# Naming the PSUM tiles of a local-attention block, and new orders for its five engines

## What is computed

```python
x = x + ga * attn_ref(layernorm(x) * (1 + ca) + sa, ...)      # causal part
h = layernorm(x) * (1 + cb) + sb
for i in range(6):                                             # the local layers
    h = attn_layer(shift_tokens(h), Wqkv[i], qs[i], ks[i], Wo[i]) + h
    h = ffn_layer(shift_tokens(h), ln_g[i], ln_b[i], W1[i], b1[i], W2[i], b2[i]) + h
return x + gb * h

# attn_layer: q, k = l2norm(.) * scale, rotary with a position scale;
#   windows of 32 keys, each query sees its own window and the one before;
#   softmax(8 q k^T) v, then @ Wo
# ffn_layer: a, gate = split(layernorm(x) @ W1 + b1); (a * gelu(gate)) @ W2 + b2
```

## Time and profile before

| | us |
|---|---|
| median of 3 runs | 3763.39 |
| the three runs | 3753.32, 3763.39, 3766.66 |
| the profiled execution, own time | 3756.22 |
| its span, first to last instruction | 3754.2 |
| PE busy | 3392.6 |
| POOL busy | 3107.4 |
| DVE busy | 2955.4 |
| ACT busy | 2601.3 |

### The profile page before, as it was taken

The page is one execution under the profiler, slowest core; times in us unless marked ns, Lnnn a source line. Parts: engine busy times, 40 slices in busy tenths (PEclk is TensorE's granted clock), DMA queues, the critical chain, the costliest instruction groups (busy, mean ns, idle before and its releaser), DMA issues.

```text
span 3754.2 us, 162428 instructions
## 1 busy us (share of the span) xinstructions
PE 3392.6 (90%) x72292; PEld 2052.2 (55%) x72292; DVE 2955.4 (79%) x3116; ACT 2601.3 (69%) x3315; POOL 3107.4 (83%) x2468
## 2 busy tenths in 40 slices
PE   7999999589998999989999889999899998989995
PEld 4666666355554555555555555555455555555553
DVE  7888887677887887878777778777788787887774
ACT  6777776467776666776677766776766777767773
POOL 3555556589998999989899988999899998989992
PEclk9999999799999999999999999999999999999997
DMA  1000000244545454545454544454444454545442
GB/s 62 5 5 8 5 5 24 75 112 114 122 107 118 95 117 108 117 109 116 93 127 108 117 100 106 114 122 105 113 102 110 116 116 106 119 95 116 104 108 80
DMA packets 162053, 347.53 MB, mean 93 GB/s; under 512 B 32588, under 2 KB 42064, under 8 KB 155088
## 3 DMA queue, kind: packets, MB, share of 16 engines
q1 hardware_dynamic: 161360, 337.15, 38.4%
HBM read 24.54 MB, written 4.19 MB: 8 GB/s over the span
## 4 chain that ended last, share of the span: by engine, by line
PE 50%; POOL 12%; DVE 7%; issue 6%; ACT 5%; SPq 1%; DMA 0%; DVEq 0%; POOLq 0%; ACTq 0%
PE psB L673 26%; PE psA L673 21%; POOL sq L1387 3%; PE psB L730 2%; DVE h L1289 2%; PE psA L730 1%; ACT sq L980 1%; POOL pb L1407 1%; POOL h L1382 1%; POOL h L1383 1%; POOL f_c L1412 1%; DVE ts L1281 1%; POOL n_a L1397 1%; POOL n_a L1394 1%; POOL n_b L1402 1%
## 5 line engine op out<-in xcount | busy, mean ns | idle before, releaser
L1362 POOL TENSOR_TENSOR pt<-wk,pt 128x256 f16<-128x256 f32 (+3 forms) x256 | 368.2, 1455 | 284.1 <-ACT pt L903 194.5
L1387 POOL TENSOR_TENSOR sq<-sq 128x512 f32<-128x512 f32 x384 | 487.3, 1281 | 82.7 <-ACT sq L980 82.4
L1382 POOL TENSOR_TENSOR h<-h,ts 128x512 f32<-128x512 f32 x384 | 503.1, 1310 | 35.3 <-DVE ts L1281 35.3
L1383 POOL TENSOR_TENSOR h<-h,ts 128x512 f32<-128x512 f32 x384 | 496.9, 1294 | 0.0
L1407 POOL TENSOR_TENSOR pb<-pb,rc 128x1024 f32<-128x1024 f32 x192 | 365.5, 1904 | 63.2 <-DVE rc L1302 60.5
L1300 DVE TENSOR_REDUCE sum<-pb 128x16 f32<-128x1024 f32 x192 | 232.9, 1213 | 108.5 <-ACT pb L1013 108.5
L1273 DVE TENSOR_TENSOR h<-psB,t_rot 128x1024 f32<-128x1024 f32 x192 | 233.6, 1217 | 77.1 <-ACT sq L980 72.6
L673 PE MATMUL psA<-kf,qf 64*32 64x64 f32 x18432 | 250.7, 227 | 29.3 <-issue 28.0
L980 ACT ACTIVATE sq<-psA 128x1024 f32<-128x1024 f32 x192 | 196.1, 1022 | 109.3 <-PE psA L673 109.2
L1273 DVE TENSOR_TENSOR h<-psA,t_rot 128x1024 f32<-128x1024 f32 x192 | 233.5, 1216 | 35.4 <-DMA kf<-h 13.9
L980 ACT ACTIVATE sq<-psB 128x1024 f32<-128x1024 f32 x192 | 196.2, 1022 | 88.2 <-PE psB L673 87.7
(11 more groups left out here) (364 smaller groups left out, 11040.7 us busy)
## 6 DMA issues: line engine op xcount, KB each, us to landing
qf<-h SPq DMA_DIRECT2D x768, 136.0 KB
kf<-h SPq DMA_DIRECT2D x768, 136.0 KB, 2.8
vev<-vo SPq DMA_DIRECT2D x192, 256.0 KB
vev<-vo SPq DMA_DIRECT2D x192, 224.0 KB
stage<-wqk SPq DMA_DIRECT2D x12, 512.0 KB, 5.3
stage<-wvl SPq DMA_DIRECT2D x12, 256.0 KB, 5.5
stage<-wof SPq DMA_DIRECT2D x6, 512.0 KB, 4.7
xb<-xt SPq DMA_DIRECT2D x8, 256.0 KB, 7.9
```

Of the source, the lines that this page charges most:

```text
L1362: e.tensor_tensor(pt[g][pr][:, :, 1, o:o + w], wk[(slot_of(s)[0] - 1) % SLOTS][:, :, 0:w], pt[g][pr][:, :, 0, o:o + w], ALU.subtract).then ...
L1382: e.tensor_tensor(halves_of(h, 0), halves_of(h, 0), t[1], ALU.subtract)
L1383: e.tensor_tensor(halves_of(h, 1), halves_of(h, 1), t[0], ALU.add).then_inc(ended["ad"])
L1387: e.tensor_tensor(sqb[c][:, 0, :], sqb[c][:, 0, :], sqb[c][:, 1, :], ALU.add).then_inc(ended["qa"])
```

## The change

Two things change.

**PSUM places.** The two rings are gone. A step now names its tile, A, B, C or D, which are psA0, psA1, psB0 and psB1. Four kinds of step that need only one bank (`ss`, `op`, `la`, `fo`) take one bank, the left (`l` or nothing) or the right (`r`), and wait only for the last users of that bank. A step that needs both banks waits for the last user of each. `plan_banks` in place of `plan_pairs` works that out, and `psum(s)` returns the bank or the pair.

**Orders.** All five tables are written anew. Nothing is added or removed: the same 2736 PE steps, 2088 of ACT, 2034 of DVE, 1536 of POOL and 492 of SP are there, in other places.

```diff
+ONE_BANK = ("ss", "op", "la", "fo")
-def plan_pairs(steps, rings):
-    at, had, place = {"A": 0, "B": 0}, {}, {}
+def plan_banks(steps, homes):
+
+    user, place = [None] * 8, {}
     for s in steps:
-        if s in rings:
-            r = rings[s]
-            slot = "AB".index(r) * 2 + at[r] % 2
-            at[r] += 1
-            place[s] = (slot, had.get(slot))
-            had[slot] = s
+        if s in homes:
+            at = 2 * "ABCD".index(homes[s][0]) + (homes[s][1:] == "r")
+            own = range(at, at + (1 if s[0] in ONE_BANK else 2))
+            place[s] = (at, sorted({user[i] for i in own if user[i]}))
+            for i in own:
+                user[i] = s
     return place
...
         def psum(s):
-            return pair[place[s][0]]
+            at = place[s][0]
+            return pair[at // 2][:, 512 * (at % 2):512 * (at % 2) + 512] if s[0] in ONE_BANK else pair[at // 2]
...
-                slot, before = place[s]
-                if before:
+                for before in place[s][1]:
...
 TENSOR = (
-    "f1:B+1 ss0:A+2 sc000:B+2 vp00:A+2 "
+    "f1:B vp01:D+1 ss0:Ar+1 sc000:B+1 vp00:D+1 sc003+1 sc002+1 sc001+1 pj10:C+1 ng00+1 sc010:A+1 sc013+1 sc012+1 "
...
 SYNC = (
-    "vd0 dm10 dm11 dm13 dm12 vd1 st1 dm00+1 dm01+1 dm03+1 st0+1 dm02+1 "
+    "dm10 st1 dm11 dm13 vd1 dm12 st0 dm00+1 dm01+1 dm03+1 dm02+1 vd0+1 "
```

More of the change, by code:

```diff
@@ L323, in program @@
         score_walk = [s for s in causal if s[0] == "c_sc"]
-        (tensor_walk, rings), (scalar_walk, _), (vector_walk, _), (gpsimd_walk, _), (sync_walk, _) = (
+        (tensor_walk, homes), (scalar_walk, _), (vector_walk, _), (gpsimd_walk, _), (sync_walk, _) = (
             walk(t) for t in (TENSOR, SCALAR, VECTOR, GPSIMD, SYNC))
@@ L330, in program @@
         count = ordinals((tensor_walk, scalar_walk, vector_walk, gpsimd_walk, sync_walk))
-        place = plan_pairs(tensor_walk, rings)
+        place = plan_banks(tensor_walk, homes)
         ts_walk = [s for s in vector_walk if s[0] == "ts"]
@@ L687, in take @@
                         e.wait_ge(*done(LAST[k], *at))
-                return pair[slot]
+                return psum(s)
             for s in tensor_walk:
```

4 lines of the change are left out of this document (2 added, 2 removed), and 20 rows, old and new, of tables (SCALAR, TENSOR, VECTOR).

## The result

The change makes the kernel slower. After it a run takes 3851.3 us in the median of four (3829.4 to 3858.0), before it 3764.3 in the same session: a ratio of 1.0227, with a 95% interval of 1.0178 to 1.0276. The forecast was 3750 with a range of 3700 to 3790, so the result lies outside it, on the other side.

A forecast was written before the change was run, and what follows sets the result against it. It took DVE's leg of 13.9 us and PE's matmuls to bound an ordinary turn. Per layer 1.1 + 1.8 + 2.0 - 3.0 = 1.9 us, ordinary turns 0, gave 3746.7 (3753.9 by median); forecast 3750, range 3700 to 3790.

The forecast's parts named there:

- The ordinary turn: Turns away from layer ends: DVE's leg and PE's matmuls stay, change 0 (-0.2 to +0.3 us), -10 to +14 over 48.
- the turns with weights ahead of `qf`: Units 70 and 72, weights fetched between in SP's queue: PE waits longer, 3.0 us a layer for both, bounds 0 and 6.
- Rival (3): Score matmuls in one piece pause PE for code: 3767 with one more pause every fourth turn, 3787 every second; chance 0.08.
- Rival (2): SP's queue: if `vd` to landing passes 9.3 us, PE waits 1 us in each of 48 turns, giving 3797; chance 0.14.
- My 7.9: SP's queue in an ordinary turn: `vd` issue 3.1, some 1.9 until the fourth `dm` starts, landing 2.8 us.
- First place: Layer end: waits ahead of `ss` and `sc` go, new ones at `pj` 3 and `op` come; gain 1.1 us, bounds 0 and 4.
- Second: A turn later: 5.0 us go at `mx` and `dm`, `ss` comes 3.1 later through `wl`; gain 1.8, bounds 0.5 and 3.5.
- 2.5 ahead of `pj` 3: In the first place: `wl`, 2.8 us, stands ahead of `bm` 3, for which `pj` 3 waits, costing 2.5 us.
- Third: A turn later still: `ow` no longer delays `pj` 1, `pj` 0 waits 1.2 behind `w1`; gain 2.0 us, bounds 0 and 3.
- the rounding of `w2`: Once-a-layer step behind `fr`: it keeps its place and its price.
- rival (1): The layer ends gain in full, most of 17.5 us a layer of waits not replaced: 3690 to 3736; chance 0.33.
- slower by over 0.5%: Whole kernel: chance 0.21, from rival (2), half of rival (3) and 0.03 of the forecast's tail.

The follow-up runs named there:

- e4: The kernel before with one move alone: `ng` 0 ahead of the first score step of group 1; ratio to before 1.0077.
- e8: After with two moves undone: `vd` behind the last `dm` of even units, `ng` 0 behind the first score of group 1; ratio to before 1.0154.
- e17: e8 with 100 do-nothing instructions on PE ahead of the local layers; ratio to before 1.0156.
- e15: The kernel before with the order of the scores inside two groups as in after; ratio to before 0.9993.
- e9: e8 with `vp` 1 of the odd unit put back between the last two `pv`; ratio to before 1.0184.
- e10: The kernel before with one move alone: `vp` 1 of the odd unit behind `f` 1; ratio to before 1.0130.
- e1: After with one SP move undone: the last `dm` of every even unit is issued ahead of `vd` again; ratio to before 1.0173.
- e7: The kernel before with only the moves of once-a-layer steps, on DVE, ACT and SP; ratio to before 0.9991.
- e11: e7 with the second `wl` of a layer moved out of DVE's leg, plus 152 do-nothing PE instructions ahead of the local layers; ratio to before 0.9928.
- e3: After with one PE move undone: `ng` 0 behind the first score step of group 1 again; ratio to before 1.0297.
- e5: The kernel before with 20 do-nothing instructions on PE ahead of the local layers; ratio to before 1.0051.
- e6: The kernel before with 152 do-nothing instructions on PE ahead of the local layers; ratio to before 0.9964.
- e18: e8 with 228 do-nothing instructions on PE ahead of the local layers; ratio to before 1.0200.
- e2: The kernel before with one SP move alone: `vd` ahead of the last `dm` of every even unit; ratio to before 1.0404.

## Why the prediction was wrong, point by point

**The ordinary turn: this term failed.** The prediction put it at 0, with -0.2 to +0.3. It measured +2.25 us. About 1.0 of that is end pauses (3.4 us a turn against 2.4), and that is the step that failed, a cost that the sum put at nothing: I had counted instructions (right) and waits, and took the pauses as a given background. About 1.2 is the wait for `qf`; 1.1 of it stands in the turns with weights ahead of `qf`, which the sum had priced by itself, at 3.0 a layer or 0.75 a turn. Of the 73 us between the two traces, end pauses are 40 to 43, depending on how the usual distance is taken. PE's busy time is 8 more (3400.9 against 3392.6), as in the mean granted clock of 0.966 where before has 0.971. The rest, some 24, is in PE's waits, and is a sum: 31 us more at the score that reads `qf`, and some 7 fewer elsewhere.

**Rival (3), denser scores, had the mechanism, at 0.08 and with too small a price.** It allowed one more pause in every fourth or second turn, 20 to 40 us. From 1000 to 3600 us after has 52 pauses in the scores where before has 22: 0.7 more a turn. One move, `ng`, costs 29 us alone (e4). The prediction set against the rule of the Trainium skill (Runtime: NRT & Kernel Launch, "Instruction fetch mechanics") that fetching is mostly hidden. The runs bear the row out, and it should have made me look for how many such places the new list has: dense runs in it are longer at the scores of group 1 and at the last two `pv`. e8 and e17 show about 37 us more than before's trace for the new list without the `ng` move. Which edits make these stays open: e15 excludes the score order, e9 and e10 are spoilt by a new wait, and a part is the two more instructions a turn, which change where packets end. So that pauses at packet ends are the largest part of the loss is shown, and that they come from denser runs is shown for `ng` alone.

**Rival (2), SP's queue, was right in kind.** Its condition was that `vd` to landing passes 9.3 us. My 7.9 took 1.9 us for four `dm` up to the start of the fourth. In the turns without weights that takes 2.8 us, so the fourth starts 6.0 us behind the first `vd`, not 5.0. With the 2.8 of the earlier trace rows the chain would be 8.8; but in the 13 such turns in which PE waited, the score came 3.5 to 4.4 us behind the start of the fourth, 9.4 to 10.6 in all. So both terms were too small, the 1.9 by 0.9 and the landing by 0.7 or more. At units 70 and 72 PE waits 4.3 and 2.6, together 6.9 against 3.0, with an upper bound of 6. The other pairs of such units within 1000 to 3600 us (22 and 24, 38 and 40, 54 and 56) gave 3.9, 3.3 and 3.5. At unit 70, `stage` lies ahead of `qf`, and by the rule of the Trainium skill (DMA: Bandwidth & Descriptors, "Queues, rings and completion order") each DMA engine takes it first. The score comes 6.0 us behind the start of the fourth `dm` there, and 4.6 to 5.0 us at units 6, 22 and 54, against the 3.5 to 4.4 without weights, so the trace agrees with the rule; no run takes the weights away to test it. From the first `vd` to the score it is 13.3 us at unit 70, above the 12.5 of the prediction, and 11.9 to 12.7 at the other three. Undone, the whole queue move is worth 0.54% by the medians (e1).

**The layer ends.** First place: the waits of 2.88 and 4.94 went, and `op` waits 2.4 to 3.8, forecast 3.6. Second: `ss` waits 3.2, forecast 3.1. The predicted 2.5 ahead of `pj` 3 is not there. Third: the wait of 1.99 went; the one of `pj` 0 behind `w1` is 2.8 to 6.0, forecast 1.2. Taken alone (e7) the three places gave 1.7 us a layer, where the steps had 4.9 (1.1 + 1.8 + 2.0). In after the four turns of a layer end got 2.2 us longer, while their end pauses grew by 4.0 (10.1 against 6.1) and their wait for `qf` by 0.5, which leaves some 2 us for the moves there too. One price that the prediction let stand changed: the wait behind the rounding of `w2` went from 4.2 to 6.1, 2 us a layer. So the mechanisms at the three places were mostly right, and rival (1), a full gain at 0.33, was far off: the rounding and the tables cost PE their time wherever they stand, save for the one `wl` that e11 found a place for.

**The signs.** I gave 0.21 to slower by over 0.5%. The zero of the ordinary turn carried the forecast, and its bounds, -10 to +14 us, were made from waits alone. The one move of `ng`, 29 us alone (e4), lies beyond them. That the result is far outside the range is thus the failure of the ordinary turn, and not bad luck at the layer ends.

## What to carry to other kernels

When a new order is weighed, look not only at who waits for whom but at how many of an engine's instructions run in how short a time. Runs of short matmuls that are cut by one long one may be cut for a reason. And an edit of an order can't be priced by undoing it alone: three of the single edits here (e3, e9, e10) only uncovered or made another wait.

A few instructions that do nothing, put where the engine waits anyway, moved this kernel by -0.4 to +0.5%. A difference of that size between two orders may be the place of their packet ends and not the order. Before such a shift is taken as a test, count the instructions of one turn: if they already spread the packet ends evenly, as here in e8, a shift changes little.

## What the runs showed of the hardware

- PE's code comes in packets of 256 instructions, 16 KB. A transfer takes 1.1 us in the mean (1.05 with the DMA engines under 5% busy, 1.10 with over 80%, so load hardly matters). At the pauses of before and after PE goes on 1.4 us behind the transfer's end (1.2 to 1.7). From the transfer's start to PE's resuming it is 2.3 to 3.1 us in nine of ten cases. The transfer starts 1.3 us behind the packet end before in the median, mostly between 0 and 4.6.
- Pauses go with short pieces. In after, of the packets of 256 instructions that PE ran in under 3 us 36 of 46 ended in a pause of over 0.3 us, of those of 3 to 4 us 38 of 82, of 4 to 6 us 26 of 192, of longer ones 9 of 166. The longest pause is 2.8 us. The 128 recorded matmuls of one score group are 256 instructions in 1.6 us.
- A sum over packet ends of 2.2 us less the time of the 160 instructions ahead, fitted on the first traces, forecast the times of e5 and e6 in sign and near size. It isn't exact: it gave 85 us of pauses for e6, which has 109, and 122, 124 and 113 for e8, e17 and e18, which have 133, 132 and 133.
- PE's granted clock in the ordinary stretches shown above is 0.98 to 1.00; in e2, with a wait of 3.6 us in the mean ordinary turn, its mean over the kernel is 0.953, against 0.971 in before.
